# Key-only piece orders for the first batch, and 14 stacking copies in place of 20

## The reference, cut to what matters

```
q, k, v = split(x @ Wqkv + bqkv)              # 16 heads of 32
q', k'  = exp(t @ omega - 0.5 * |t|^2)        # 128 features per head
k_sum   = sum over rows of k';  k_v = k'^T v  # over a whole batch
out     = (q' @ k_v) / (q' @ k_sum + 1e-6)    # then @ Wout + bout
y       = layernorm(x + out)
z       = layernorm(y + y @ weight^T + pooled(y) @ disha)
```

## Time and profile before

| | |
|---|---|
| median of 3 executions | 2633.75 us (2627.39 to 2639.04) |
| span of the profiled execution, first to last instruction | 2625.4 us |
| median less span, what lies around it | 8.4 us |
| TensorE busy | 2449.6 us (93%) |
| DVE, ACT, GpSimd busy | 77%, 42%, 20% |
| mean granted TensorE clock | 0.982 |

### The profile page before, as it was taken

How to read it: one execution, slowest core, us unless ns; L and a number is a source line. 1 busy time by engine, 2 the same in 40 slices (tenths; PEclk the granted TensorE clock), 3 DMA queues, 4 the chain that set the end, 5 groups by cost and what they waited for, 6 DMA issues and landing times.

```text
span 2625.4 us, 64569 instructions
## 1 busy us (share of the span) xinstructions
PE 2449.6 (93%) x24576; PEld 1402.6 (53%) x24576; DVE 2012.5 (77%) x3966; ACT 1114.5 (42%) x1921; POOL 513.1 (20%) x522
## 2 busy tenths in 40 slices
PE   4888999999999999999999999999999999997776
PEld 2445555555555555555555555555555555553333
DVE  5446788888887888787887888878887878877675
ACT  1444444444443444444444444435444444442321
POOL 2010221222211122212212221112222122121111
PEclk9898999999999999999999999999999999999998
DMA  4222333233223323323332332332333233222220
GB/s 165 62 66 62 99 86 83 78 95 94 75 82 87 84 77 95 95 59 99 87 86 75 94 84 73 95 84 79 86 94 95 59 99 87 79 74 58 58 57 33
DMA packets 85263, 214.96 MB, mean 82 GB/s; under 512 B 19312, under 2 KB 21456, under 8 KB 80720
## 3 DMA queue, kind: packets, MB, share of 16 engines
q1 hardware_dynamic: 84944, 210.63, 29.0%
HBM read 74.24 MB, written 33.55 MB: 41 GB/s over the span
## 4 chain that ended last, share of the span: by engine, by line
PE 85%; DVE 8%; issue 3%; ACT 2%; SPq 1%; DMA 1%; POOL 0%; DVEq 0%; POOLq 0%; ACTq 0%
PE bank_y L365 23%; PE bank_a L365 23%; PE bank_x L365 12%; PE bank_kf L405 4%; PE bank_qf L449 4%; PE bank_x L478 4%; PE kv_ps L423 2%; PE kv_ps L428 2%; PE bank_nm L465 2%; PE bank_nm L467 2%; PE bank_nm L466 2%; PE kv_ps L426 2%; DVE k_feat_lo L660 2%; PE bank_x L375 1%; PE bank_a L375 1%
## 5 line engine op out<-in xcount | busy, mean ns | idle before, releaser
L777 POOL TENSOR_TENSOR rstd<-mean_var,minus_half 128x1 f32<-128x1 f32 x256 | 166.8, 652 | 1770.8 <-DVE mean_var L615 1770.8
L534 ACT ACTIVATE k_feat<-bank_kf 128x512 f32<-128x512 f32 x512 | 305.7, 597 | 253.0 <-PE bank_kf L405 239.6
L660 DVE TENSOR_TENSOR k_feat_lo<-k_feat 128x512 bf16<-128x512 f32 x512 | 362.6, 713 | 60.6 <-ACT k_feat L534 54.7
L667 DVE TENSOR_TENSOR q_feat_lo<-q_feat 128x512 bf16<-128x512 f32 x512 | 355.4, 704 | 29.9 <-ACT q_feat L543 26.7
L543 ACT ACTIVATE q_feat<-bank_qf 128x512 f32<-128x512 f32 x512 | 305.5, 597 | 164.9 <-PE bank_qf L449 138.7
L549 ACT ACTIVATE at_hi<-bank_x 128x512 f16<-128x512 f32 x128 | 76.4, 597 | 396.6 <-PE bank_x L478 396.6
L365 PE MATMUL bank_a<-xt_hi,wqkv_hi 128*128 128x512 f16 x480 | 187.6, 391 | 46.4 <-POOL xt_lo L759 26.0
L423 PE MATMUL kv_ps<-v_hi,k_feat 128*128 128x33 f16 x2048 | 208.3, 179 | 11.4 <-DVE k_feat_lo L660 9.9
L405 PE MATMUL bank_kf<-omega_s,stack_k 98*128 98x128 f16 x2048 | 200.6, 220 | 17.4 <-ACT k_feat L534 14.9
L449 PE MATMUL bank_qf<-stack_q,omega_s 98*128 98x256 f16 x1024 | 197.0, 274 | 15.4 <-ACT q_feat L543 15.2
L365 PE MATMUL bank_y<-wffn_hi,yt_hi 128*128 128x512 f16 x512 | 195.7, 382 | 16.3 <-DVE yt_lo L715 14.5
(11 more groups left out here) (116 smaller groups left out, 6078.4 us busy)
## 6 DMA issues: line engine op xcount, KB each, us to landing
xt_f<-xt SPq DMA_DIRECT2D x33, 1024.0 KB, 5.0
stack_k<-t_hi_k SPq DMA_DIRECT2D x256, 128.0 KB
stack_q<-t_hi_q SPq DMA_DIRECT2D x256, 128.0 KB
rows<-x SPq DMA_DIRECT2D x128, 256.0 KB, 2.8
out<-rows SPq DMA_DIRECT2D x128, 256.0 KB, 2.0
stack_k<-t_lo_k SPq DMA_DIRECT2D x128, 128.0 KB
stack_q<-t_lo_q SPq DMA_DIRECT2D x128, 128.0 KB
stack_k<-half_norm SPq DMA_DIRECT2D x256, 4.0 KB
```

The costliest lines, as they stand in the source:

```text
L534: nc.scalar.activation(k_feat[:, i % 2, :], bank_kf[:, :], ACT.Exp, scale=1.0 / WS).then_inc(S["k_exp"], 1)
L660: v.tensor_tensor(k_feat_lo[:, u, :], k_feat[:, u, :], k_feat_hi[:, u, :], ALU.subtract).then_inc(S["kfl"], 1)
L667: v.tensor_tensor(q_feat_lo[:, at, :], q_feat[:, at, :], q_feat_hi[:, at, :], ALU.subtract).then_inc(S["qfl"], 1)
```

## The change

1. ORDER_K is a new text for the first three slots of the first batch, and ORDER_FIRST is rewritten and serves the fourth alone. In ORDER_K, four KF and three KV of a chunk stand in its own slot and the rest in the next, where it had been seven and six. KN stands behind the first half of VP0 and not before it.
2. In those three slots the key norms go to bank_x.
3. A stack is made with 14 copies: 4 + 4 of the hi parts, which wait only for k_hi and kf_done, then 4 of the lo part behind k_lo, then 2 norm copies, one for each norm row. For this the norms of the 16 heads are spread over partitions 0, 8, 16, ... (NORM_STEP), and the stack is laid out by group and then head in a group, as [P, G, HPG, CHUNK] and not [P, HPG, G, CHUNK]. This cuts the copies of t_hi and t_lo into runs of 512 elements (1 KB), where a partition had one run of 4 KB.

```
-MOVES = 16 * (3 * HPG + 2 * G)
+NORM_STEP = P // H
+MOVES = 16 * (3 * HPG + 2)

 ORDER_FIRST = """
-KP0. KF7' KP0 KV6' KF8' KP1. KFIN' KV7' KF9' KP1 KV8' KF10' KV9' KP2. KF11' KP2 KF12' KV10' KP3.
-KV11' KF13' KP3 KV12' KF14' KV13' KF15' KV14' QP0. QP0 KN VP0. QP1. QP1 VP0 QP2. KV15' QP2 VP1. VP1
-VP2. QP3. XS QP3 VP2 KF0 KF1 VP3. KV0 KF2 VP3 KV1 KV2 KF3 KF4 KV3 KF5 KF6 KV4 KV5
+KP0. KF4' KP0 KV3' KF5' KP1. KFIN' KV4' KF6' KP1 KV5' KF7' KP2. KV6' KF8' KP2 KV7' KF9' KP3. KV8' KF10'
+KP3 KV9' KF11' QP0. KV10' KF12' QP0 KV11' KF13' KN KV12' KF14' KV13' KF15' KV14' QP1. KV15' QP1 VP0. VP0
+VP1. VP1 QP2. QP2 VP2. VP2 XS QP3. QP3 KF0 VP3. KF1 KV0 VP3 KF2 KV1 KF3 KV2 KV3 KF4 KF5 KV4 KF6 KV5
+"""
+
+ORDER_K = """
+KP0. KF4' KP0 KV3' KF5' KP1. KV4' KF6' KP1 KV5' KF7' KP2. KV6' KF8' KV7' KF9' KP2 KV8' KF10' KP3. KV9' KF11'
+KV10' KF12' KP3 KV11' KF13' KV12' KF14' VP0. KV13' KF15' KV14' KN VP0 KV15' VP1. VP1 VP2. VP2 XS KF0
+VP3. KF1 KV0 VP3 KF2 KV1 KF3 KV2
 """
...
-SP_ORDERS = 3 * [pieces("""
+SP_ORDERS = 4 * [pieces("""
...
-        stack = {s: sb(f"stack_{s}", [P, HPG, G, CHUNK], F16) for s in "kq"}
+        stack = {s: sb(f"stack_{s}", [P, G, HPG, CHUNK], F16) for s in "kq"}
...
-                return bank_y if isinstance(b, int) and b == 0 and kind != "KN" and i % 2 else bank_a
+                if isinstance(b, int) and b == 0:
+                    return bank_x if kind == "KN" and shared(b, c) else bank_a if kind == "KN" else bank_y if i % 2 else bank_a
+                return bank_a
...
+        def order_at(b, c):
+
+            if not isinstance(b, int):
+                return 1
+            return 3 if b < 0 or b == 0 and c < CPB - 1 else 0 if b == 0 else 2 if b >= B else 1
+
+        def shared(b, c):
+
+            return order_at(b, c) == 3
...
-                wait(sp, f"{s}_lo", G * (n + 1))
+                def rows_of(row, t):
+                    for j in range(HPG):
+                        sp.dma_start(stack[s][DH * row:DH * (row + 1), :, j, :],
+                                     t[DH * j:DH * (j + 1), :, :]).then_inc(S[name], 16)
+
+                wait(sp, f"{s}_hi", G * (n + 1))
                 carry()
                 wait(sp, f"{s}f_done", 16 * n)
-                for j in range(HPG):
-                    for row, t in enumerate((t_hi[s], t_lo[s], t_hi[s])):
-                        sp.dma_start(stack[s][DH * row:DH * (row + 1), j, :, :],
-                                     t[DH * j:DH * (j + 1), :, :]).then_inc(S[name], 16)
+                rows_of(0, t_hi[s])
+                rows_of(2, t_hi[s])
+                wait(sp, f"{s}_lo", G * (n + 1))
+                rows_of(1, t_lo[s])

             def stack_norms(s, n, name):

                 wait(sp, f"{s}n_lo", n + 1)
-                for g in range(G):
-                    for r in range(2):
-                        sp.dma_start(stack[s][96 + r:97 + r, :, g, :],
-                                     half_norm[32 * g:32 * g + HPG, r, :]).then_inc(S[name], 16)
+                for r in range(2):
+                    sp.dma_start(stack[s][96 + r:97 + r, :, :, :].rearrange("p g j n -> p (g j) n"),
+                                 half_norm[0:P:NORM_STEP, r, :]).then_inc(S[name], 16)
...
-                v.memset(norm_w[DH * j:DH * (j + 1), j:j + 1], -0.5).then_inc(S["dve_const"], 1)
+                v.memset(norm_w[DH * j:DH * (j + 1), NORM_STEP * j:NORM_STEP * j + 1], -0.5).then_inc(S["dve_const"], 1)
```

More of the change, by code:

```diff
@@ L99, in later @@
     return [p for _, p in sorted(keyed, key=lambda x: x[0])]
-PE_ORDERS = [pieces(text) for text in (ORDER_FIRST, ORDER, ORDER_LAST)]
+PE_ORDERS = [pieces(text) for text in (ORDER_FIRST, ORDER, ORDER_LAST, ORDER_K)]
 ENDED = [[p for p in order if p[2] != "first"] for order in PE_ORDERS]
@@ L222, in runs @@
             return not isinstance(b, int) or 0 <= chunk_of(b, c, kind, back) < B * CPB
-        def order_at(b):
-            return 1 if not isinstance(b, int) else 0 if b <= 0 else 2 if b >= B else 1
+        def order_at(b, c):
[4 more added lines that the diff above has]
+            return order_at(b, c) == 3
         def slots(eng, orders, step):
             def slot(b, c):
-                for kind, i, what, back in orders[order_at(b)]:
+                for kind, i, what, back in orders[order_at(b, c)]:
                     if runs(b, c, kind, back) and (kind != "KFIN" or (c - back) % CPB == CPB - 1):
@@ L343, in bank_free @@
             def bank_free(b, c, kind, i):
-                bank = bank_of(b, kind, i)
-                order = ENDED[order_at(b)]
+                bank = bank_of(b, c, kind, i)
+                order = ENDED[order_at(b, c)]
                 at = next(n for n, p in enumerate(order) if p[:2] == (kind, i))
@@ L352, in bank_free @@
                         where = b + there // CPB if isinstance(b, int) else b
-                        if k in FREED and bank_of(where, k, n) is bank and runs(b, there, k, back):
+                        if k in FREED and bank_of(where, there % CPB, k, n) is bank and runs(b, there, k, back):
                             name, per = FREED[k]
@@ L357, in bank_free @@
                     there -= 1
-                    order = ENDED[order_at(b + there // CPB if isinstance(b, int) else b)]
+                    order = ENDED[order_at(b + there // CPB if isinstance(b, int) else b, there % CPB)]
             def twelve(bank, parts, what, done):
@@ L371, in _, with norms @@
             yt_p, wf_p = [{"hi": yt_hi[:, u, :, :], "lo": yt_lo[:, u, :, :]} for u in range(2)], {"hi": wffn_hi, "lo": wffn_lo}
-            def norms(done):
+            def norms(bank, done):
                 for g in range(G):
-                    last = nc.tensor.matmul(bank_x[32 * g:32 * (g + 1), :] if done == "qn_done" else
-                                            bank_a[32 * g:32 * (g + 1), :],
+                    last = nc.tensor.matmul(bank[32 * g:32 * (g + 1), :],
                                             norm_w[:, :], squares[done[0]][:, g, :], start=True, stop=True,
@@ L387, in step @@
                         bank_free(b, c, kind, i)
-                    twelve(bank_of(b, kind, i), lambda kb, s, m: (w3[s][:, kb, D + P * i:D + P * (i + 1)],
+                    twelve(bank_of(b, c, kind, i), lambda kb, s, m: (w3[s][:, kb, D + P * i:D + P * (i + 1)],
                                                      xt_p[m][:, c % CPB, kb, :]), what, "kp_done")
@@ L392, in step @@
                         bank_free(b, c, kind, i)
[L393 removed]
+                    twelve(bank_of(b, c, kind, i), lambda kb, s, m: (xt_p[s][:, c % CPB, kb, P * i:P * (i + 1)],
                                                      w3[m][:, kb, 2 * D:3 * D]), what, "vp_done")
@@ L397, in step @@
                     bank_free(b, c, kind, i)
-                    norms("kn_done")
+                    norms(bank_of(b, c, kind, i), "kn_done")
                 elif kind == "KF":
@@ L405, in step @@
                         last = nc.tensor.matmul(bank_kf[:, M * jj:M * (jj + 1)],
-                                                stack["k"][0:STACK, jj, g, P * t:P * (t + 1)],
+                                                stack["k"][0:STACK, g, jj, P * t:P * (t + 1)],
                                                 omega_s[0:STACK, :], start=True, stop=True)
@@ L440, in step @@
                     bank_free(b, c, kind, i)
-                    norms("qn_done")
+                    norms(bank_of(b, c, kind, i), "qn_done")
                 elif kind == "QF":
@@ L449, in step @@
                         last = nc.tensor.matmul(bank_qf[:, HALF * e:HALF * (e + 1)], omega_s[0:STACK, :],
-                                                stack["q"][0:STACK, hh // G, hh % G,
+                                                stack["q"][0:STACK, hh % G, hh // G,
                                                            HALF * half:HALF * (half + 1)],
@@ L512, in step @@
                 if kind == "KP":
-                    project("k", bank_of(b, kind, i), kA, i, G)
+                    project("k", bank_of(b, c, kind, i), kA, i, G)
                     if i == 0:
@@ L517, in step @@
                             wait(act, "kfin", b)
-                    square("k", bank_of(b, kind, i), i, G)
+                    square("k", bank_of(b, c, kind, i), i, G)
                 elif kind == "QP":
@@ L528, in step @@
                     nc.scalar.activation(v_hi[:, i, :, 0:DH],
-                                         bank_of(b, kind, i)[:, :].rearrange("p (h d) -> p h d", d=DH),
+                                         bank_of(b, c, kind, i)[:, :].rearrange("p (h d) -> p h d", d=DH),
                                          ACT.Copy).then_inc(S["v_hi_done"], 1)
@@ L642, in step @@
                 if kind == "KP":
-                    t_low("k", bank_of(b, kind, i), kA, i, G)
+                    t_low("k", bank_of(b, c, kind, i), kA, i, G)
                 elif kind == "QP":
@@ L646, in step @@
                 elif kind == "KN":
```

(2 more changed lines are left out.)

3 lines of the change are left out of this document (1 added, 2 removed).

## The result

The changed kernel takes 2623.08 us (median of 7 executions, 2611.06 to 2623.87), the kernel before 2634.84 us (7 executions beside it, 2627.39 to 2639.04). The ratio is 0.9951, 95% interval 0.9937 to 0.9966: 11.8 us less by the medians, 9 to 17 by the interval. Forecast were 2622 and 11.4 us less.

The account below looks back on a forecast made before the run. TensorE, busy 93% of the span, was taken as the bound, with idle time and low clock to recover in the first four slots. 11.1 us there plus 0.3 off 2633.75 gave 2622; eight in ten 2613 to 2634.

Parts of the forecast that it names:

- up to 0.5 us for the small pieces: Stack copies: allowance for a later landing because each 128 KB copy goes in 1 KB pieces.
- The walk: First four slots, followed piece by piece at full clock: 30.8 + 37.0 + 37.0 + 51.0 = 155.8 us.
- The 0.3 us for QF0: Slot (1,0): QF0 lands on its norms' heels in the old trace; a gain of 0.3 us was given.
- three drops: First batch: three stretches of low clock, 1.7 us each, 5.1 us in all, of a possible 0 to 6.
- Rival 1: First three slots: waits cost less clock or copies land earlier; 19 us less, 2614; gain above 13 us: chance 0.38.
- Rival 3: Stack copies: 1 KB pieces are dear, KF0 4.6 us later in three slots; 2636, no change; chance 0.12.
- Rival 4: All 28 middle slots: a copy's pitch passes 1.13 us and KF0 waits; 2673 to 2721; chance 0.05.
- 15.8 us of copies: Middle slots: the 14 copies may take up to this long, 1.13 us each, before KF0 waits.
- 0.7 us over 12: Stack copies: cost estimated from the port rule for four copies in a row to the same 32 partitions.
- my 0.69: Stack copies: us per copy, estimated from the port rule's 189 GB/s for partitions 0 to 31.
- the base: Whole kernel: timed median 2633.75 us, 8.4 above the profiled span of 2625.4; start and end unchanged.
- the one that the prediction names: Last five slots: one with TensorE busy 48.48 of 64.60 us, said to lose as much as the first ones.

Follow-up runs that it names:

- e7: The changed kernel once more, with nothing altered; 2622.09 us, ratio 0.9954 to the kernel before.
- e1: New piece orders and bank_x for the key norms, with the old 20 copies per stack and old stack layout; 2633.96 us, ratio 0.9998 to before.
- e2: Old piece orders with the new 14 copies per stack; 2630.74 us, ratio 0.9990 to the kernel before.
- e3: The changed kernel with 8 norm copies in place of 2, so 20 copies with 1 KB pieces; 2635.47 us, ratio 1.0002 to before.
- e4: The changed kernel with VP3's first half moved in front of KF0 in ORDER_K; 2620.99 us, ratio 0.9949 to before.
- e6: The changed kernel with VP3's first half ahead of KF0 in ORDER_K and ORDER_FIRST mended for chunk 3; 2616.20 us, ratio 0.9931 to before.
- e8: The changed kernel with 4 more copies per stack, of 8 partitions each, into rows no matmul reads; 2633.62 us, ratio 0.9999 to before.
- e9: The changed kernel with 12 more copies per stack, of eight partitions each, into rows no matmul reads; 2836.90 us, ratio 1.0775 to before.
- e10: The changed kernel with its 14 copies in the old alternation of high and low parts, behind one wait; 2625.12 us, ratio 0.9964 to before.
- e5: The changed kernel with the first three slots' key norms back in bank_a and KN before VP0; 2630.38 us, ratio 0.9985 to before.

## Why the prediction was right, step by step

**The gain and its place.** Forecast were slots of 31 to 33, 37 to 39, 37 to 39 and 51 to 53 us, slot (1,0) at 187 and the middle at 75.0; measured 33.4, 38.3, 38.3, 51.7, 187.59 and 75.00. Forecast for the first batch were 11.1 us less; 10.4 came, and 11.8 in the medians. In e7 it is 13.0 in the slots and 12.7 in the medians. e1 and e2 show that both halves are needed. That the sum came so close is in part luck: two errors of 2.5 us cancel, as told below under the clock.

**Chunk 0: two terms too small, with one sum.** KF0 was to come at 50.2 to 50.7 after a wait of 2.1; it came at 51.97 after 3.80. The start of the copies (39.98 for 40.1) was right. Their issue took 10.4 us instead of 8.9: the four low copies took 3.75 us, against 2.54 in chunk 1, 1.2 too many. e1, e3, e4, e6, e7, e8, e9 and e10 have such an excess too, of 0.6 to 1.2 us, in a copy that SP issues between 47 and 50 us; e2 and e5, whose copies were all issued by 48.5, and the kernel before have none. What it is stays open. And the landing was 1.6 instead of 1.2 us, in all three slots.

**Landing.** I allowed up to 0.5 us for the small pieces and put 1.2 into the sum. The 0.4 came, but e3 shows that the small pieces aren't its cause; what is left between the two kernels is the two larger norm copies.

**Chunks 1 and 2.** The walk gave 37.0 at full clock; e7, at a clock of 1.00, has 37.60. KF15' gates the copies: they leave 20.2 us into the slot, 20.4 were forecast, issued in 9.1 (8.9), and the wait before KF0 is 2.55 in TensorE's rows (2.3). Of the 0.6, 0.4 are landing and pitch, which bring KF0 30.9 us into the slot instead of 30.5; the other 0.2 lie in the pieces and waits around it. e5 confirms the gate from the other side.

**Chunk 3 and slot (1,0).** 51.0 forecast at full clock, 51.7 measured at 0.95. These don't agree as well as they look: 4.7 us of the slot ran at half the clock (from 159.0 and 186.3). e5's chunk 3, with the same text and the first of the two stretches missing, takes 50.1, so at full clock the walk is too long by about 1 us or more. It has 8.5 us of waits there, and TensorE is idle for 6.0 (51.68 less 45.71). The 0.3 us for QF0 didn't show: slot (1,0) is 71.4 before and after.

**The clock.** "I take three drops, 5.1 us, of a possible 0 to 6": the profile has exactly three in the first three slots, one behind each wait for the stack (from 53.2, 90.7 and about 128, granted clock 0.50). That it was three is luck in part: e7 has none there with the same waits. And the price was wrong. Three stretches were to cost 5.1 us, 1.7 each; between e7, which has none, and the profile they cost 1.3, 0.7 and 0.7, 2.7 together. Against that, the walk of the first three slots at full clock was too short: 104.8 us (30.8 + 37.0 + 37.0), where e7 has 107.3. The one error is 2.4 us too much, the other 2.5 too little. The two stretches in chunk 3 stood in no sum. Why a stretch costs less than half its length there isn't shown (in chunk 3 it cost 1.5, by e5); behind KF0 TensorE waits for ACT and DVE between the pieces (idle for 0.66 and 0.44 at 134.76 and 135.59), and such waits can take up what the slower clock loses.

**The rivals.** Rival 1 (no drops, 2614) wants a stack that lands earlier; e4 and e7 have each a part of it, and e7's profiled execution, without a drop in the first three slots, took 2621.12, so the clock alone doesn't reach it. Rival 3 (dear 1 KB pieces, 2636) falls by the pitch of 0.65 and the DMA share of 28.9%. Rival 4 (every middle slot waits) didn't happen, with 7.5 us of cover in a middle slot, and e9 shows that its mechanism is real. Its bound, 15.8 us of copies, is only bracketed: e8, whose eighteen take 12.0, leaves the middle at 75.0, and e9, whose twenty-six take 17.9, pays in every slot. With what e9 measured for the loads (1.30) and the landing (2.64) the bound is an estimated 14.1, and e9 lies 3.8 over it, near its wait of 4.1. By my bound it was 2.1 over, priced at 2 to 4 us a slot, and it cost 6.5.

**Small pieces, and rows to the same ports.** By the Trainium skill (DMA: Bandwidth & Descriptors, Why small descriptors are slow (HBM only)) transfers from SBUF to SBUF don't suffer from small pieces. The trace agrees: 28.9% against 29.0%, and a landing of 1.14 us against 1.15. By the Trainium skill (SBUF: State Buffer, Door 1: The DMA port swizzle) a transfer to partitions 0 to 31 reaches half of the ports. From it I had estimated that the new order of copies costs 0.7 us over 12. e10 shows none of it, and the estimate didn't follow from the rule, which speaks of one transfer: the 128 KB copies write 32 partitions each in both orders, so it makes no difference between them. The rule isn't refuted by that. At 0.65 us a copy they move 202 GB/s in either order, so my 0.69 was too dear as well.

**The steps that failed.** One is the price of a stretch of low clock, 1.7 us for a measured 0.7 to 1.3, which hid that the first three slots were walked too short. The other is the base: "the three timed ones have the median 2633.75, 8.4 above; the start (26.04, setup) and the end don't change". Only 1.7 us lie around a span. Most of the other 6.7, an estimated 6.2, lay in the last batch of that execution, where the clock fell less (285.2 us for the 291.4 of the changed kernel's profile). In the total it did no harm, because I took the difference from the median of the runs; had I added 11.4 to the span, the two spans (3.7 us apart) would have looked like a miss. A reading was off too, with nothing resting on it: the last five slots don't lose as much each as the first four, but more, 16.1 us of idle TensorE in the one that the prediction names, against 5.7 to 8.8.

## What to carry to other kernels

When an operand is assembled by many DMAs from one queue, count the copies before their bytes: here each held the queue for 0.63 to 0.65 us, whether 4 KB or 128 KB (0.73 for 32 KB to eight partitions), and six fewer turned an order that gave nothing (e1) into 11 us. An order that takes waits away from one engine must be walked to the next gate (here KF15', then the last copy), since both halves alone gave 0 and 4 us. And read a gain of a few us from the slots that the change touches, not from two spans: the last five slots, with the same text, differed by 6 us between two executions. What a stretch of low clock costs is best read from two executions of one kernel, slot by slot: here it was 0.7, 0.7 and 1.3 us, where half the stretch is 1.7.

## What was not expected of the hardware

- The same wait of 2.55 us of TensorE was followed by 3.4 us at a granted clock of 0.50 (1.2 GHz) in one execution and by none in another of the same kernel, 2.7 us over three slots.
- A norm copy of 16 KB, from 16 partitions to one, lets the matmul behind it start 1.59 us after its issue; one of 4 KB, 1.14.
- A copy of 32 KB to eight partitions costs SP 0.73 us, more than one of 128 KB to 32 partitions (0.65).
- The same two norm copies let KF0 start 1.58 us after their issue in e9's first slot and 2.64 us after it in a middle slot, where two loads of rows are issued just ahead of them. That the loads are the cause isn't shown by a run of its own.
